# A fused cross-attention and quantised feed-forward kernel: the context is laid out as columns by four transfers into quadrants and VectorE's block transpose in place of TensorE transposes

## What is computed

```python
def xattn(q, k, v, ...):                       # H = 16 heads of 32
    query = q @ w_q.T + b_q; key_ = k @ w_k.T + b_k; value = v @ w_v.T + b_v
    scores = where(causal, einsum('bhqd,bhkd->bhqk', query, key_) / sqrt(32), -inf)
    x = einsum('bhqk,bhkd->bhqd', softmax(scores), value)
    return merge_heads(x) @ w_o.T + b_o
def ffn(x, weight, bias):                      # blocks of 32: scale = max|block| / 7.5
    return dequantised(fp6_grid(x)) @ dequantised(fp6_grid(weight)).T + bias
x = x + tanh(g_xattn) * xattn(layernorm(x), ctx, ctx)
x = x + tanh(g_ffn) * ffn(layernorm(x))
```

## Time and profile before

| | |
|---|---|
| Time, median of 3 runs | 1406.31 us (1406.27 to 1407.74) |
| The profiled execution | 1405.65 us, of which its span is 1403.9 us |
| PE busy | 1368.0 us (97%) |
| DVE, ACT, POOL busy | 1085.5, 896.8, 867.0 us |
| Chain that ended last | PE 91%; SP's queue 3%; DVE 2% |
| Granted TensorE clock, mean | 0.990 of full speed |
| Context transfer, median | 5.9 us from issue to landing |

### The profile page before, as it was taken

One profiled execution on the slowest core, in us unless ns is written; L12 is line 12 of the kernel. 1 busy time (PEld: TensorE's weight loads), 2 busy tenths in 40 slices (PEclk: granted clock), 3 DMA queues, 4 the chain that ended last, 5 costly groups with the idle time before them and its releaser, 6 DMA issues.

```text
span 1403.9 us, 35217 instructions
## 1 busy us (share of the span) xinstructions
PE 1368.0 (97%) x10844; PEld 1221.2 (87%) x10844; DVE 1085.5 (77%) x4219; ACT 896.8 (64%) x2969; POOL 867.0 (62%) x1387
## 2 busy tenths in 40 slices
PE   6899999999999999999999999999999999999987
PEld 6789988899888898898898988889998888998875
DVE  5777787887787887778777778878778878778774
ACT  4666666666666666666667666666666566666562
POOL 1556765566665576665566666566666566666564
PEclk9999999999999999999999999999999999999998
DMA  8444344444334444434444434454434444434320
GB/s 254 112 112 116 88 115 118 120 128 114 98 102 122 118 125 117 111 95 121 118 128 118 112 90 119 118 131 119 111 89 121 118 125 123 112 97 112 88 68 31
DMA packets 156616, 159.11 MB, mean 113 GB/s; under 512 B 28688, under 2 KB 131088, under 8 KB 156432
## 3 DMA queue, kind: packets, MB, share of 16 engines
q1 hardware_dynamic: 156432, 156.88, 42.0%
HBM read 39.33 MB, written 16.78 MB: 40 GB/s over the span
## 4 chain that ended last, share of the span: by engine, by line
PE 91%; SPq 3%; DVE 2%; issue 1%; DMA 1%; POOL 1%; ACT 1%; DVEq 0%; ACTq 0%; POOLq 0%
PE proj L511 20%; PE proj L512 20%; PE proj L513 20%; PE pT_ps L572 12%; PE proj L588 6%; PE proj L615 6%; PE s_ps L561 4%; PE s_ps L562 2%; SPq L360 2%; DMA all_probs<-in_L_xattn_w_v 1%; DMA q_stack<-q_hi 0%; DMA k_stack<-k_lo 0%; POOL xs_yz L472 0%; POOL xs_yz L476 0%; ACT all_probs L691 0%
## 5 line engine op out<-in xcount | busy, mean ns | idle before, releaser
L437 POOL TENSOR_TENSOR all_probs<-all_probs,rden 128x128 f32<-128x128 f32 (+1 forms) x1024 | 517.6, 526 | 445.9 <-DVE rden L895 444.5
L691 ACT ACTIVATE all_probs<-all_probs,neg_max 128x128 f32<-128x128 f32 (+1 forms) x1024 | 458.8, 451 | 373.0 <-DVE neg_max L837 372.7
L837 DVE CUSTOM_DVE_ANT_0 all_probs<-s_ps,causal 128x128 f32<-128x128 f32 (+1 forms) x1024 | 323.6, 353 | 195.7 <-PE s_ps L562 190.0
L572 PE MATMUL pT_ps<-ident,all_probs 128*128 128x128 f32 x1536 | 264.4, 282 | 7.8 <-POOL all_probs L437 4.0
L691 ACT ACTIVATION_READ_ACCUMULATOR all_probs<-all_probs,neg_max 128x1 f32 x1024 | 195.4, 191 | 0.0
L959 DVE COPY all_probs<-pT_ps 128x384 f32<-128x384 f32 x256 | 139.2, 544 | 53.8 <-PE pT_ps L572 53.5
L572 PEld LDWEIGHTS pT_ps<-ident,all_probs 128*128 128x128 f32 x1536 | 160.4, 142 | 22.8 <-issue 12.5
L561 PE MATMUL s_ps<-k_stack,q_stack 96*128 96x256 f32 x512 | 154.5, 302 | 3.3 <-DVE neg_max L837 2.2
L511 PE MATMUL proj<-cT_hi,wk_hi 128*128 128x256 f32 x512 | 153.6, 300 | 0.0
L511 PE MATMUL proj<-aT_hi,wq_hi 128*128 128x256 f32 x512 | 148.6, 290 | 0.0
L512 PE MATMUL proj<-aT_lo,wq_hi 128*128 128x256 f32 x512 | 142.9, 279 | 0.0
(11 more groups left out here) (114 smaller groups left out, 3465.1 us busy)
## 6 DMA issues: line engine op xcount, KB each, us to landing
k_stack<-k_hi SPq DMA_DIRECT2D x512, 64.0 KB, 2.0
q_stack<-q_hi SPq DMA_DIRECT2D x512, 64.0 KB, 2.1
xs_yz<-in_x SPq DMA_DIRECT2D x32, 512.0 KB, 4.5
cs<-in_ctx SPq DMA_DIRECT2D x32, 512.0 KB, 5.9
k_stack<-k_lo SPq DMA_DIRECT2D x256, 64.0 KB, 2.0
q_stack<-q_lo SPq DMA_DIRECT2D x256, 64.0 KB, 2.1
out<-xs_yz SPq DMA_DIRECT2D x64, 256.0 KB, 2.3
vs<-in_L_xattn_w_k SPq DMA_DIRECT2D x2, 512.0 KB, 7.0
```

What stands on the lines that cost most here:

```text
L437: last = nc.gpsimd.tensor_tensor(p, p, rden[:, sd, t, h:h + 1].to_broadcast([P, (1 + t) * P]), ALU.mult)
L572: last = nc.tensor.transpose(pT_ps[h % 2][:, m * P:(m + 1) * P], probs[:, h % P_RING, m * P:(m + 1) * P], ident[:, :])
L691: last = nc.scalar.activation(probs[:, h % P_RING, cols], probs[:, h % P_RING, cols], ACT.Exp, scale=-1.0, bias=neg_max[:, sd, t, h:h + 1] ...
L837: last = nc.vector.tensor_tensor_reduce(probs[:, h % P_RING, cols], s_ps[h % 2][:, cols], causal[:, (1 - t) * P:], 1.0, MASKED, ALU.add, A ...
```

## The change

TensorE's transposes of the context are gone (the units cT, eight instructions for each batch). Instead:

- SP loads the context of batch i by four transfers into `c_quads`, one for each quadrant of 32 partitions: quadrant g gets features g*128 to g*128+127 of all tokens, in runs of 512 bytes, with 32 tokens on the 32 partitions.
- DVE turns 32x32 blocks (`turn`, in slots 5 and 9 of step i, one call for 128 tokens) into `cols`. Feature 4p + c comes to stand on partition p in chunk c; so the weights of k and v are transposed with a stride of four columns.
- ACT rounds `cols` to `cT_hi` (slots 6 and 10), POOL subtracts for `cT_lo` (slots 7 and 12) in place of DVE. `cT_hi` and `cT_lo` have two places, for even and odd batches.
- The parts of the 14 units that are left are spread anew over the slots, the first layernorm goes from slot 6 to 15, its power on POOL to slot 0 of the next step, `XB_SLOTS` to (5, 6), `XN_SLOTS` to (1, 3), the feed-forward bias one slot earlier.

```diff
-UNITS = [("cT", 0, 1), ("cT", 1, 1), ("q", 1, 2), ("dT", 0, 4), ("k", 0, 1), ("dT", 1, 4), ("f", 0, 4), ("xT", 0, 1),
+UNITS = [("q", 1, 2), ("dT", 0, 4), ("k", 0, 1), ("dT", 1, 4), ("f", 0, 4), ("xT", 0, 1),
          ("f", 1, 4), ("xT", 1, 1), ("o", 0, 3), ("o", 1, 3), ("q", 0, 1), ("v", 0, 1), ("k", 1, 1), ("v", 1, 1)]
...
-SLOT_PARTS = (2, 4, 4, 1, 1, 5, 4, 2, 3, 4, 4, 1, 3, 3, 3, 2)
+SLOT_PARTS = (3, 3, 3, 1, 3, 4, 4, 3, 3, 3, 3, 1, 3, 3, 3, 1)
...
-XB_SLOTS = (9, 12)
-LN1_SLOT = 6
-XN_SLOTS = (2, 3)
+XB_SLOTS = (5, 6)
+LN1_SLOT = SLOTS - 1
+XN_SLOTS = (1, 3)
+QUAD = 32
+TURN_SLOTS = (5, 9)
+C_HI_SLOTS = (6, 10)
+C_LO_SLOTS = (7, 12)
...
+            def context(b):
+
+                for g in range(NQ):
+                    sp.dma_start(c_quads[g * QUAD:(g + 1) * QUAD, :, :],
+                                 ctx_in[b, :, g * P:(g + 1) * P].rearrange("(n l) d -> l n d", l=QUAD)).then_inc(
+                                     c_in, 16)
...
                     sp.dma_start(xs[:, place(ph, 0), :, :], batch_of(x, i)).then_inc(x_in, 16)
-
-                    if some(n := 2 * i):
-                        sp.wait_ge(done["cT"], n)
-                    sp.dma_start(cs[:, :, :], batch_of(ctx_in, i)).then_inc(c_in, 16)
+                    if i:
+
+                        sp.wait_ge(turned, 2 * i)
+                        context(i)
...
+            def context_lo(b, t):
+
+                pool.wait_ge(chi_ok, 2 * b + t + 1)
+                tok = slice(t * P, (t + 1) * P)
+                nc.gpsimd.tensor_tensor(cT_lo[:, b % 2, :, tok], cols[:, t, :, :], cT_hi[:, b % 2, :, tok].bitcast(F32),
+                                        ALU.subtract).then_inc(clo_ok, 1)
...
+                    if s in C_LO_SLOTS and live(i):
+                        context_lo(i, C_LO_SLOTS.index(s))
+                    if s == 0 and i > 1 and live(i - 1):
+                        deviation_in(i - 1)
...
+                elif w in "kv" and c == 0:
+
+                    for arrived in raw_in[w]:
+                        pe.wait_ge(arrived, 16)
...
+                cols = slice(c, D, KC) if w in "kv" else slice(c * P, (c + 1) * P)
...
-                        pe.wait_ge(left[src], 2 * b + 2)
+                        pe.wait_ge(left["xT"] if kind == "q" else clo_ok, 2 * b + 2)
...
+            def context_hi(b, t):
+
+                act.wait_ge(turned, 2 * b + t + 1)
+                if some(n := 2 * (b - 1)):
+
+                    act.wait_ge(done["k"], n)
+                    act.wait_ge(done["v"], n)
+                nc.scalar.activation(cT_hi[:, b % 2, :, t * P:(t + 1) * P], cols[:, t, :, :],
+                                     ACT.Copy).then_inc(chi_ok, 1)
...
+            def turn(b, t):
+
+                dve.wait_ge(c_in, 16 * NQ * (b + 1))
+                if some(b):
+
+                    dve.wait_ge(clo_ok, 2 * (b - 1) + t + 1)
+                nc.vector.transpose(cols[:, t, :, :].rearrange("p c (n l) -> p n c l", l=QUAD),
+                                    c_quads[:, t * NQ:(t + 1) * NQ, :].rearrange("p n (e c) -> p n c e",
+                                                                                c=KC)).then_inc(turned, 1)
```

67 lines of the change are left out of this document (36 added, 31 removed).

## The result

The changed kernel takes 1431.89 us (median, 1430.97 to 1433.83) against 1406.29 us (1406.09 to 1407.74) of the kernel before beside it. The ratio is 1.0182 with an interval of 1.0170 to 1.0195: slower by 25.6 us, where I had forecast 20 us faster. The profiled execution has a span of 1432.0 us against 1403.9.

The account below looks back on a forecast made before the run. PE alone was taken to set the steady pace. Its saving, start, two step 2 terms and late contexts gave -26.1 + 1.3 + 1.2 + 0.5 + 3 = -20.1 us, hence 1386 us, range 1377.5 to 1400.

Parts of the forecast that it names:

- PE's saving: Context transposes gone from PE: 0.87 us a step, 26.1 us over steps 3 to 32, step 40.96 us.
- The cost of these two is nothing: Added DVE turns and POOL subtractions stay covered in each step, with turns up to about 3.5 us; cost nothing.
- The tables only move such pieces: Respreading PE's units over the slots costs PE nothing, so the step falls from 41.83 to 40.96 us.
- T: Length of one DVE block transpose of the context: 0.6 to 0.7 us, bounds 0.5 to 1.84.
- The arrival: Context lands 15.5 to 16 us after the step's first scores; some steps stall PE, 3 us in all.
- rival 1: Context arrives late in each step, stalling PE 1.3 us; 1422 us, slower; chance 9%.
- rival 1's half: Smaller stalls from the late context, 0.3 to 0.7 us a step; 1392 to 1404 us; chance 17%.
- My deciding point: Context arrival + T above 16.7 us into the step costs PE the excess; above 17.6 the change loses.
- k_hi's wait: ACT waits about 2 us for k_stack in slot 3 each step, 60 us in all, at no cost.
- The start: Later weight loads delay the feed-forward weight's POOL passes: +1.3 us; v's transposes at 24.5 to 25.5 us.
- The tail: Steps after the last batch of keys: nothing gained or lost.
- Rival 3: Another handoff, POOL's cluster in slots 11 to 15 and 0, is as late as PE; 1403 to 1407; chance 3%.

Follow-up runs that it names:

- e6_turns: e5_both with the context's second half turned in slot 6, rounded in 7 and its remainder taken in 8, not 9, 10 and 12; 1395.28 us.
- e7_tail: e6_turns with the old slot table of the kernel before in steps 33 and 34; 1391.54 us, ratio 0.9894.
- e12_v_first: e7_tail with k's weight loaded between the context and x, and v's ahead of the feed-forward weight; 1391.71 us.
- e4_nocontext: Changed kernel without the context's transfers, turns, roundings and subtractions from batch 2 on, reusing the first two batches' columns; 1412.55 us.
- e11_oldtable: Changed kernel with its 14 units spread over the slots by the table of the kernel before; 1433.28 us.
- e2_early: Changed kernel with the next context's transfers issued earlier, between the first pair's k_stack and q_stack; 1418.63 us.
- e1_xn: Changed kernel with the first half of the normalised rows in slot 2 instead of slot 1; 1430.17 us.
- e10_rows: Changed kernel with the context loaded as whole tokens in runs of 2 KB instead of 512 bytes, same bytes; 1422.94 us.
- e3_start: Changed kernel with both halves of batch 1's context turned in slot 5 and rounded in slot 6 of step 1; 1426.87 us.
- e5_both: Changed kernel with the edits of e1_xn and e2_early together; 1406.54 us.

## Why the prediction was wrong

**PE's saving: right.** The steps without a stall last 40.98 us in e6_turns, e7_tail and e12_v_first; I had 40.96. The 0.87 us of the transposes was the right number, and not eight times the group's mean of 0.277 us. The Trainium skill (VectorE: DVE Perf Modes, section The three transpose paths) has 390 ns for one such transpose on TensorE, in bf16; the step's floor falls by 41.82 - 40.98 = 0.84 us, 105 ns for each of the eight float32 ones, and agrees with the 109 ns read from the rows instead.

**"A head's reciprocal and division are done at least 1.3 us before PE transposes it, so both stay covered ... The cost of these two is nothing": this step failed, and with it "The tables only move such pieces".** I checked one handoff, the division to the transposes, and only for the length T of the turn. Three things were missing:
- The product with values needs the copy of head 15, and that copy stands on ACT behind the exponentials of head 2, these behind DVE's maxima, these behind whatever DVE has in slot 1. I had listed the layernorm's move to slots 15, 0 and 1 as part of the change and then costed it at nothing. It cost 3.17 - 2.48 = 0.69 us a step, 20 us in 29 steps. Its slack was in the trace of before (0.8 us, between 672.79 and 673.58) and I didn't write it down. Nor did I ask what xn would meet in its new place: beside GpSimd's dequantisation it takes 1.26 us, and not 0.53.
- T is 1.10 us, not 0.6 to 0.7. I took the nearest row in size, an elementwise pass; my bounds (0.5 to 1.84) held it. The second half of the context, turned in slot 9, cost slot 11 0.17 us a step (e4_nocontext, e6_turns), 5 us.
- That the table's pieces cost PE nothing was right in the steady part and wrong in the tail, where its slot 2 is empty: 5.8 us of the tail in the changed kernel (e11_oldtable), 3.5 in the repaired one (e6_turns to e7_tail), the lower clock included.

**The arrival: the mechanism right, the term too small; it is the second one that failed.** DVE waited 43 us in 30 times where I had 30 us in all. The turn that waited began 15.7 to 17.8 us after its step's first scores, 16.6 on average, where I had 15.5 to 16. The first transfer went out at 9.80 us in the step shown (8.8 to 10.5 over the steady steps), not at 9.1, and the last of four landings came 7.1 us after that, at the median, where the single transfer took 5.9. The stalls in slots 5 and 6 came to 0.38 us a step (against e2_early's slots) where I had 0.1: 8 us more in all, of the size of rival 1's half. But slot 3's wait hid the rest. My deciding point, arrival + T above 16.7, was exact: without that wait (e1_xn) slot 6 grows from 15.60 + 1.10 = 16.70 on. At 16.6 + 1.10 = 17.7 the context was beyond even the 17.6 that I had named for a change that loses, and e1_xn, with slot 3 mended and the context late, is no faster than the changed kernel by more than its scatter. Either fault alone was enough to lose the forecast. The Trainium skill (DMA: Bandwidth & Descriptors, section Specifications) puts full rate at 512 bytes and more. By it e10_rows should have changed nothing. The trace disagrees: at equal bytes the last landing comes 0.7 us earlier with runs of 2 KB, and the kernel gained 8.9 us.

**k_hi's wait: right.** 62.6 us against 60, and hidden in the changed kernel in all steps but one, where it reaches 4.3 us and slot 5 lasts 4.48 us and not 3.05. In the repaired kernels, where the steps are shorter, it grows to 80 to 91 us and is the next bound.

**The start: +1.3 us forecast, +6.8 found.** K's wait for cT_lo in step 2 came as I said (2.1 us). V's transposes came at 26.23, not at 24.5 to 25.5. What I missed is DVE's and ACT's order in step 1: the second turn behind the 2.27 us pass, its rounding copy ahead of v's weights. PE's wait of 3.48 us for them is half of the 6.8, and e3_start removes it. For the feed-forward pass on GpSimd, on which I had hung the start, PE doesn't wait at all there.

**The tail: nothing forecast, 7.6 us found.** The old table alone takes 5.8 us of it away (e11_oldtable). Without it e1_xn has 0.7 us less, e2_early 1.1 and both together 3.6; how these share it with the clock is not shown.

**The sum.** Against the forecast span of 1383.8 us the changed kernel is 48 us late: 33 us in steps 4 to 32 (20 from slot 3, 8 from the arrival, 5 from slot 11), 5.5 at step 2's start, 2 in steps 2 and 3, and 7.6 in the tail. (The 20 and 8 are what e5_both's two edits remove together; singly they don't add up, as above.) e7_tail undoes most of these four. Its profiled span is 1387.4 us, 3.6 above the 1383.8: its step 2 still starts 1.6 us later than I had it, step 3 is 1.1 us longer and the tail 1.4, and the steady steps are 0.5 us shorter in all. Its median, 1391.5 us, is 5.5 above my 1386. The mechanism of the gain was sound; the change as made hides it behind handoffs that it moved itself.

**The chances.** I gave 9% to slower, and that only through the arrival (rival 1). Its condition was met, 17.7 us against 17.6, but by a T of 1.10 more than by slow packets. Its time, 1422 us, was not met, since slot 3, slot 11, the start and the tail came on top. Rival 3, another handoff as late as PE, had 3%, because I looked for it in the busy shares (DVE 159, POOL 129 of 200 us). Those shares say nothing of a chain that passes PE, DVE, ACT and PE within 3 us.
